# Layer 0's mixture of experts: PSUM banks dealt out anew between the first-layer products and everything else

## The chip, the cores and the metric

The kernel runs on one NeuronCore of a Trainium2 chip. The metric is the device time of one execution in microseconds (us). Engines are named as the profile names them: PE is TensorE (PEld its weight loads), DVE is VectorE, ACT is ScalarE, POOL is GpSimd, SP is SyncE, which issues the DMAs. PSUM has eight banks of 512 float32 columns; TensorE writes them, VectorE and ScalarE read them.

## What is computed

The program is four layers, each an attention part and a feed-forward part with a layer norm before it and a residual after it, on 4096 rows of 128 values. The change touches layer 0's feed-forward part, a mixture of 16 experts on small tokens (each row is 8 tokens of 16 values):

```python
h = x @ Wm + bm
t = h.reshape(bs * L_ * H, HD)                 # 32768 tokens of 16
logits = t @ expert_emb                        # 16 experts
w = jax.nn.softmax(logits, axis=-1)
topw, topi = jax.lax.top_k(w, K)               # K = 2
hmid = jax.nn.gelu(jnp.einsum('td,edi->tei', t, W1) + b1, approximate=False)
eo = jnp.einsum('tei,eio->teo', hmid, W2) + b2
sel = jnp.take_along_axis(eo, topi[:, :, None], axis=1)
comb = (sel * topw[:, :, None]).sum(axis=1)
out = comb.reshape(bs, L_, d)
return out @ Wo + bo
```

## The kernel before

All 16 experts are computed for all tokens, and the gates (zero for the experts that a token did not choose) weight them. The 4096 rows are eight batches of 512 (`NB = 8`, batch `b`). A batch is 8 steps `n` (so `n` runs over 64), and a step is four units `i = 4n + c`. `order()` writes the stage as one list that every engine follows; a step has four slots. The work around the change:

- **mm1** (L248 to L257), one per unit: two bfloat16 matmuls of 512 columns into a pair of PSUM banks. It waits until the GELU of unit i-2 is done, since there are two pairs, banks 0 and 1 and banks 2 and 3. In slot s of step n stands mm1 of unit 4n+5+s.
- **gelu** (L265), one per unit: ScalarE turns a pair of banks into an SBUF buffer (its name in the rows is p1g, xn or xT, by the storage that is used).
- **comb** (L547), two per step, in slots 0 and 1: eight rows of float32 matmuls in four column groups, into bank 4 for the first and bank 5 for the second. It needs all four GELUs of the step, and the bank's last content read.
- **the gating** (L582), one per comb: VectorE reads the comb's bank, adds b2, multiplies by the gates, and so frees the bank.
- **red** (L555), two per group of four steps: matmuls that sum the gated rows, into bank 6. Two groups accumulate in bank 6 and one VectorE copy (L588) takes them out for each batch. Red stands in slot 2 of steps with n % 4 equal to 0 and 1, one in each.
- **finish** (L565, then L188): the product with Wo in bank 7 and VectorE's addition to X.
- **the routing of a batch** ("side" work, a generator with one piece in each slot and two in the first four steps): the transposes *turn* (L179), copy (L299), *wm* (L403), VectorE's *hT* (L306) and the three-part split of h (L309 to L319), *lg* (L409), the maximum and difference (L322, L326), ScalarE's exp (L428), some 13 VectorE operations that find the top two and make the gates (L329 to L376, called rank 0 to 10 after the change), *gateT* (L416) and its copy (L382). All of it goes through bank 7, and turn, the next batch's turn and finish wait for one another there.

Batches 0 and 1 differ. Batch 0's routing is done during layer 0's attention: its loop has 12 rounds, and rounds 4 to 11 each take four pieces (`step(side, 4)`). Rounds 9 to 11 also issue mm1 of units 0 to 6. Batch 1's routing runs at two pieces per slot in steps 0 to 3.

The two lines of mm1 that hold the turnover, and the three of order():

```python
        b, hp, ep, ka = n // 8, n % 4, 4 * (n // 4 % 2) + c, 2 * (i % 2)
        p.wait_ge(k.sem("gelu"), i - 1)
...
                if 7 <= 4 * n + 5 + slot < 256:
                    yield "mm1", 4 * n + 5 + slot
                elif slot == 2 and n > 3 and n % 4 < 2:
```

Of the kernel before, what the change touches and what calls it, by code (L numbers as in the profile page):

```python
# [15 lines left out]
NB = 8  # L16
# [7 lines left out]
def _layout(specs):  # L24
# [166 lines left out]
class Mixture:  # L191
# [3 lines left out]

    def __init__(self, k, ctx):
# [15 lines left out]
        self.gscr = [k.nc.dram_tensor(f"gscr{i}", [128, 512], F32).ap() for i in range(2)]  # L212

# [45 lines left out]
    def gelu(self, a, i):  # L259
        k, ka, ep = self.k, 2 * (i % 2), 4 * (i // 16 % 2) + i % 4  # L260
# [19 lines left out]
    def batch_vector(self, v, b):  # L280
        k, i, at = self.k, b % 2, 4 * (b % 4)
# [15 lines left out]
        v.wait_ge(k.sem("proj"), 3 * b + 3 if b < 4 else 24)
        v.wait_ge(k.sem("wm"), b - 3)
        v.e.tensor_copy(k.xT[:, 128 * at:128 * at + 512], k.ps[:, 7, :]).then_inc(k.sem("xT1").h, 1)  # L299
        yield  # L300
        yield
        yield
        v.wait_ge(k.sem("w", 1), 16)
        v.wait_ge(k.sem("wm"), b + 1)
        v.wait_ge(k.sem("lg"), b - 1)
        v.e.tensor_scalar(hT[:, :], k.ps[:, 7, :], k.Wt(1, "bm"), None, ALU.add).then_inc(k.sem("hT").h, 1)  # L306
        v.wait_ge(k.sem("hT"), b + 1)
        v.wait_ge(k.sem("ts", i), 48 * (b // 2))
        v.e.tensor_copy(tp[0][:, :], hT[:, :]).then_inc(k.sem("tp").h, 1)  # L309
        yield  # L310
        yield
        v.wait_ge(k.sem("tp"), 3 * b + 1)
        v.e.tensor_tensor(tr[:, :], hT[:, :], tp[0][:, :], ALU.subtract).then_inc(v.own.h, v.one())
        tb = v.n
        yield
        v.wait_ge(v.own, tb)
        v.e.tensor_copy(tp[1][:, :], tr[:, :]).then_inc(k.sem("tp").h, 1)
        v.wait_ge(k.sem("tp"), 3 * b + 2)
        v.e.tensor_tensor(tp[2][:, :], tr[:, :], tp[1][:, :], ALU.subtract).then_inc(k.sem("tp").h, 1)  # L319
        yield  # L320
        v.wait_ge(k.sem("lg"), b + 1)
        v.e.tensor_reduce(m1[:, :], lg, AX, ALU.max).then_inc(v.own.h, v.one())  # L322
        t = v.n
        yield
        v.wait_ge(v.own, t)
        v.e.tensor_tensor(D[:, :, :], lg, bc(m1), ALU.subtract).then_inc(k.sem("D").h, 1)  # L326
        yield
        v.wait_ge(k.sem("D"), b + 1)
        v.e.scalar_tensor_tensor(U[:, :, :], D[:, :, :], 0.0, rev, ALU.is_equal, ALU.mult).then_inc(v.own.h, v.one())  # L329
        t = v.n  # L330
        yield
        v.wait_ge(v.own, t)
# [2511 lines left out]
```

## Time and profile before

| | |
|---|---|
| median of 3 runs | 1707.63 us (1703.91 to 1710.57) |
| the profiled execution's own time | 1705.46 us |
| its span, first to last instruction | 1703.7 us |
| mean granted TensorE clock | 0.943 |
| steps 6 to 53 of the stage (start of the first gating of step 6 to that of step 54) | 145.34 to 423.45, 278.11 us |
| starts of the first gatings of steps 55 to 59 | 428.33, 433.21, 438.24, 443.27, 448.15 |
| steps 8k to 8k+3 of the six batches k = 1 to 6 | 22.56, 24.15, 22.56, 24.14, 24.15, 22.56 us |
| stage from the first gating to that of step 63 | 102.51 to 469.78, 367.27 us |

The profile is of one execution. The page gives busy time and its share by engine and in 40 slices; a view by windows gives busy time between two moments; the timeline gives single instructions. A gating (L582) stands once for each comb, so its start times mark the steps. A matmul row's length includes the pipeline's drain, so two starts, not a length, tell how long it keeps PE.

### The profile page before, as it was taken

The numbers are of one execution on the slowest core, as the hardware profiler recorded it, in microseconds if no ns is written. First come the engines' busy times: TensorE is split into PE (matmuls) and PEld (weight loads), VectorE is DVE, ScalarE is ACT, GpSimd is POOL, SyncE is SP. The second block draws the span as 40 slices with busy tenths as digits, with TensorE's granted clock in tenths as the row PEclk, the third lists the DMA queues.
The fourth block names the chain that finished last, engine by engine and source line by source line (L and its number), as shares of the span: only waits on it lengthen the run. The fifth ranks groups of instructions, "written<-read, shape, count | busy, mean of one in ns | idle before, by whom it ended". The sixth has DMA issues, their size and how long they took to land.

```text
span 1703.7 us, 22900 instructions
## 1 busy us (share of the span) xinstructions
PE 1456.3 (85%) x8197; PEld 655.3 (38%) x8235; DVE 1332.1 (78%) x2813; ACT 1040.7 (61%) x1903; POOL 337.0 (20%) x270
## 2 busy tenths in 40 slices
PE   6568898888867867799999999999999898895756
PEld 3522222222246656333333333333333334563645
DVE  7765656666365867788888899888888669998997
ACT  4457878888843121577777787777777675361332
POOL 3000000000011332011111111111111124544554
PEclk9789999999997989999999999999999988898877
DMA  3155545455210010100000000000000000000001
GB/s 88 27 123 123 133 126 132 121 132 132 75 47 1 11 54 1 62 1 1 1 1 1 1 13 13 1 1 1 1 1 1 25 1 1 1 1 0 7 13 31
DMA packets 44657, 64.13 MB, mean 38 GB/s; under 512 B 5376, under 2 KB 26112, under 8 KB 44160
## 3 DMA queue, kind: packets, MB, share of 16 engines
q1 hardware_dynamic: 44544, 62.67, 13.8%
q8 instruction: 65, 1.06, 0.3%
q14 instruction: 48, 0.39, 0.1%
HBM read 54.27 MB, written 7.34 MB: 36 GB/s over the span
## 4 chain that ended last, share of the span: by engine, by line
PE 52%; DVE 26%; issue 11%; ACT 8%; POOL 2%; DMA 1%; SPq 0%; DVEq 0%; POOLq 0%; ACTq 0%
PE ps L1959 11%; PE ps L1950 8%; PE ps L547 6%; PE ps L256 6%; PE ps L1929 4%; DVE p6ac L2501 3%; PE ps L1969 3%; DVE WA L2535 3%; DVE xn L172 2%; PE ps L1939 2%; ACT p1g L265 2%; PE ps L555 1%; PE ps L687 1%; DVE st L154 1%; DVE X L188 1%
## 5 line engine op out<-in xcount | busy, mean ns | idle before, releaser
L2046 ACT ACTIVATE p4E<-ps,p4mx,p4sc 128x512 f32<-128x512 f32 x512 | 392.7, 774 | 138.2 <-DVE p4mx L2005 138.2
L2003 DVE TENSOR_REDUCE p4mx<-ps 128x2 f32<-128x1024 f32 x256 | 312.5, 1221 | 63.7 <-PE ps L1950 61.5
L1959 PE MATMUL ps<-p4E,p4vn 128*64 128x512 f32 x1024 | 249.6, 608 | 9.2 <-POOL p4vn L2064 9.1
L1950 PE MATMUL ps<-p4T 64*128 64x512 f16 x1536 | 200.2, 380 | 3.9 <-ACT p4E L2046 3.2
L582 DVE SCALAR_TENSOR_TENSOR p1Pb<-ps,WB,p1sh 128x512 f32<-128x512 f32 x128 | 96.0, 750 | 131.3 <-PE ps L547 127.0
L256 PE MATMUL ps<-p1R,p1w1s 128*128 128x512 bf16 x474 | 142.4, 392 | 43.9 <-ACT p1g L265 22.2
L166 POOL TENSOR_TENSOR rs<-rs,cst 128x4 f32<-128x4 f32 x58 | 59.9, 1033 | 561.6 <-DVE rs L160 561.6
L2064 POOL TENSOR_TENSOR p4vn<-p4v,p4zs 128x512 f32<-128x512 f32 x64 | 66.7, 1043 | 496.5 <-DVE p4zs L2008 496.5
L265 ACT ACTIVATE p1g<-ps,WB 128x1024 f32<-128x1024 f32 x128 | 136.6, 1113 | 43.6 <-PE ps L256 43.5
L547 PE MATMUL ps<-p1g,WB 128*32 128x512 f32 x512 | 138.3, 629 | 0.0
L547 PE MATMUL ps<-xn,WB 128*32 128x512 f32 x256 | 137.5, 621 | 0.0
L1959 PEld LDWEIGHTS ps<-p4E,p4vn 128*64 128x64 f32 x1024 | 63.6, 136 | 137.0 <-issue 136.9
L1950 PEld LDWEIGHTS ps<-p4T 64*128 64x128 f16 x1536 | 58.9, 94 | 140.5 <-ACT p4E L2046 80.8
L256 PEld LDWEIGHTS ps<-p1R,p1w1s 128*128 128x128 bf16 x512 | 36.4, 99 | 193.3 <-issue 73.7
L1929 PE MATMUL ps<-xT,WA 128*128 128x512 f16 x384 | 104.8, 382 | 2.4 <-DVE X L188 0.9
L2038 ACT ACTIVATE p4T<-ps,p4qkb 128x512 f16<-128x512 f32 x128 | 88.0, 689 | 25.7 <-PE ps L1929 25.0
L2046 ACT ACTIVATION_READ_ACCUMULATOR p4E<-ps,p4mx,p4sc 128x1 f32 x512 | 100.4, 196 | 0.0
L1988 DVE SCALAR_TENSOR_TENSOR p4T<-ps,p4qkb,p4T 128x512 f16<-128x512 f32 x128 | 95.3, 745 | 1.8 <-ACT p4T L2038 1.8
L172 DVE TENSOR_SCALAR xn<-X,mv,rs 128x128 f32<-128x128 f32 x232 | 78.6, 394 | 10.1 <-POOL rs L166 10.0
L188 DVE TENSOR_TENSOR X<-X,ps 128x512 f32<-128x512 f32 x66 | 45.0, 683 | 50.5 <-PE ps L565 16.0
L265 ACT ACTIVATE xT<-ps,WB 128x1024 f32<-128x1024 f32 x64 | 70.9, 1115 | 20.1 <-PE ps L256 20.1
L265 ACT ACTIVATE xn<-ps,WB 128x1024 f32<-128x1024 f32 x64 | 68.9, 1112 | 15.1 <-PE ps L256 15.1
(358 smaller groups left out, 2691.5 us busy)
## 6 DMA issues: line engine op xcount, KB each, us to landing
p1sh<-gscr SPq DMA_DIRECT2D x128, 256.0 KB
p1R<-tscr SPq DMA_DIRECT2D x64, 128.0 KB, 5.2
tscr<-p1tp SPq DMA_DIRECT2D x24, 128.0 KB, 1.7
WA<-in_w SPq DMA_DIRECT2D x1, 2632.0 KB, 8.9
WB<-in_w SPq DMA_DIRECT2D x1, 2560.0 KB, 8.8
X<-in_x SPq DMA_DIRECT2D x8, 256.0 KB, 5.8
gscr<-p1gT SPq DMA_DIRECT2D x8, 256.0 KB, 2.0
out<-X SPq DMA_DIRECT2D x8, 256.0 KB, 2.3
```

Source lines behind the costliest of these rows:

```text
L172: v.e.tensor_scalar(self.xn[:, at + j, :], self.X[:, i, :], self.mv[:, i, 0:1], self.rs[:, i:i + 1], ALU.subtract, ALU.mult).then_inc(self ...
L256: t = p.e.matmul(k.ps[:, ka + hh, :], self.w1s[:, 128 * ep:128 * ep + 128], self.R[b % 2][:, 2 * hp + hh, :], start=True, stop=True)
L265: a.e.activation(self.gb[i % 8], k.ps[:, ka:ka + 2, :].rearrange("p a c -> p (a c)"), ACT.Gelu, bias=k.Wt(1, "b1")[:, ep:ep + 1]).then_inc ...
L547: p.e.matmul(k.ps[32 * c:32 * c + 32, 4 + hh, :], k.Wt(1, "w2")[:, 32 * ep:32 * ep + 32], self.gb[i % 8][:, 512 * hh:512 * hh + 512], star ...
L582: v.e.scalar_tensor_tensor(self.Pb[m % 12][:, :], k.ps[:, 4 + hh, :], k.Wt(1, "b2")[:, half:half + 1], self.GB[n % 4][:, hh, :], ALU.add, ...
L1929: t = p.e.matmul(ps[:, self.bank[what, x], :], pre.part(("kw", "qw")[x[1]], r, slice(128 * hp, 128 * hp + 128)), halves(k, b)[q], start=o ...
L1950: y = p.e.matmul(ps[:, at + hh, :], t[rows, q, 128 * j:128 * j + 128], t[rows, 2 + r, :], start=o == 0, stop=o == 2)
L1959: t = p.e.matmul(ps[64 * hh:64 * hh + 64, 7, :], vn[n % 2][:, j, 64 * hh:64 * hh + 64], E[2 * (n % 2) + hh][:, j, :], start=j == 0, stop=j ...
L1988: v.e.scalar_tensor_tensor(t[:, 2 * c + 1, :], ps[:, self.bank["kq", x], :], pre.qkb[:, 1 - c, hp:hp + 1], t[:, 2 * c, :], ALU.add, ALU.su ...
L2003: v.e.tensor_reduce(m, ps[:, at:at + 2, :], AX, ALU.max).then_inc(v.own.h, v.one())
L2038: a.e.activation(T[n % 2][:, 2 * c, :], ps[:, self.bank[what, x], :], ACT.Identity, bias=pre.qkb[:, 1 - c, n % 8:n % 8 + 1]).then_inc(k.se ...
L2046: a.e.activation(self.E[2 * i + hh][:, j, :], ps[:, at + hh, :], ACT.Exp, bias=self.mx[i][:, j, hh:hh + 1], scale=pre.sc[:, 1, 0:1], accum ...
```

## The change

Units' products get a third pair of banks, 6 and 7: mm1 and gelu use `PAIRS = (0, 2, 6)[i % 3]`, mm1 waits for the GELU of unit i-3, and stands one unit earlier in the list (slot s of step n has unit 4n+6+s). Everything else in the stage (comb, red, turn, wm, lg, gateT, finish, the next layer's turn) takes banks 4 and 5 in turn, in the order in which TensorE meets them: use u goes to bank 4 + u % 2, and waits (`released`) until VectorE has taken out use u-2. For that the side pieces are named and listed (`batch_steps`), and the list is public to all engines.

With it: a red group is closed by itself (bank taken out each group; the second group's is added to the first's in SBUF by a VectorE tensor_tensor), and both reds of a group stand in slots 2 and 3 of the step with n % 4 == 0. Side pieces come ahead of the slot's comb, not behind it. The routing order moves a little: the logits' maximum and difference stand before parts 1 and 2 of the split, and the statistics of the next batch's norm come one step later. Batch 0's routing inside the attention takes its 24 pieces in rounds 4 to 7 (`first`), four non-empty entries in each, where it had rounds 4 to 11; its PSUM uses go to bank 6, and so mm1 of unit 2 waits for batch 0's `gT`.

```diff
+    PAIRS = (0, 2, 6)
...
+        self.bank = {(what, 0): 6 for what in ("turn", "wm", "lg", "gateT")}
+        self.bank.update({u: 4 + i % 2 for i, u in enumerate(uses)})
+        self.last = {u: uses[i - 2] for i, u in enumerate(uses) if i > 1}
...
     def mm1(self, p, i):
-        b, hp, ep, ka = n // 8, n % 4, 4 * (n // 4 % 2) + c, 2 * (i % 2)
+        b, hp, ep, ka = n // 8, n % 4, 4 * (n // 4 % 2) + c, self.PAIRS[i % 3]
-        p.wait_ge(k.sem("gelu"), i - 1)
+        if i % 3 == 2:
+            p.wait_ge(k.sem("gT"), 1)
+        p.wait_ge(k.sem("gelu"), i - 2)
...
+    STEPS = (("rows", 0), ("turn", 3), ("xT", 1), ("wm", 1), ("hT", 0), ("lg", 2), ("logits", 0), ("parts 0", 1), ("parts 1", 0),
+             ("exp", 1), ("rank 0", 0), ("rank 1", 1), ("rank 2", 1), ("rank 3", 0), ("rank 4", 0), ("rank 5", 1), ("rank 6", 0),
+             ("rank 7", 3), ("rank 8", 0), ("rank 9", 1), ("rank 10", 2), ("gateT", 5), ("gT", 0))
...
+    def first(self, n):
+        steps = [labels for labels in self.batch_steps(0) if labels]
+        for labels in steps[4 * n:4 * n + 4 if n < NB - 1 else None]:
+            yield from labels
...
     def order(self):
+        side = self.batch_steps(1)
         for n in range(64):
             for slot in range(4):
-                if 7 <= 4 * n + 5 + slot < 256:
-                    yield "mm1", 4 * n + 5 + slot
+                if 7 <= 4 * n + 6 + slot < 256:
+                    yield "mm1", 4 * n + 6 + slot
+                for _ in range(2 if n < 4 else 1):
+                    yield from next(side, ())
                 if slot < 2:
                     yield "comb", (n, slot)
-                elif slot == 2 and n > 3 and n % 4 < 2:
-                    yield "red", (n // 4 - 1, n % 4)
-                yield "side", 2 if n < 4 else 1
+                elif n > 3 and n % 4 == 0:
+                    yield "red", (n // 4 - 1, slot - 2)
...
+    def released(self, p, use):
+        if use not in self.last:
+            return
+        what, x = self.last[use]
+        if what == "comb":
+            p.wait_ge(k.sem("gated"), 2 * x[0] + x[1] + 1)
+        elif what == "red":
+            p.wait_ge(k.sem("cT"), x + 1)
+        elif what == "turn":
+            p.wait_ge(k.sem("xT1"), x + 1)
+        elif what == "wm":
+            p.wait_ge(k.sem("hT"), x + 1)
+        elif what == "lg":
+            p.wait_ge(k.sem("D"), x + 1)
+        elif what == "gateT":
+            p.wait_ge(k.sem("gT"), x + 1)
...
             elif what == "red":
                 g, hh = x
+                if hh == 0:
+                    self.released(p, (what, g))
                 p.wait_ge(k.sem("gated"), 8 * g + 7 + hh)
-                p.wait_ge(k.sem("cT"), g // 2)
-                               start=g % 2 == 0 and hh == 0, stop=g % 2 == 1 and hh == 1, skip_group_check=True)
+                               start=hh == 0, stop=hh == 1, skip_group_check=True)
...
+                v.wait_ge(k.sem("red"), 8 * g + 8)
+                if g % 2 == 0:
+                    v.wait_ge(k.sem("y1"), g // 2 - 1)
+                    v.e.tensor_copy(cT, k.ps[:, bank[what, g], :]).then_inc(k.sem("cT").h, 1)
+                else:
+                    v.wait_ge(k.sem("cT"), g)
+                    v.e.tensor_tensor(cT, k.ps[:, bank[what, g], :], cT, ALU.add).then_inc(k.sem("cT").h, 1)
...
-                step(side, 4)
+                for what, x in self.mix.first(b):
+                    self.mix.batch_vector(v, what, x)
```

## Rows read from the trace of the kernel before

**Rows 1.** The page: busy us and share of the span; PE's granted clock by slice.

```profile
PE 1456.3 (85%) x8197; PEld 655.3 (38%) x8235; DVE 1332.1 (78%) x2813; ACT 1040.7 (61%) x1903; POOL 337.0 (20%) x270
...
PEclk9789999999997989999999999999999988898877
```

**Rows 2.** Windows: length, busy us by engine (instructions), PE's clock, DMA share, GB/s.

```profile
62.00:102.50 40.50, 27.53 (x171) 22.26 (x172) 28.82 (x63) 9.24 (x9) 2.29 (x2) 0.83 0.31 60
102.51:145.34 42.83, 31.59 (x173) 8.02 (x170) 26.57 (x57) 27.18 (x27) 3.31 (x3) 0.92 0.56 146
145.34:423.45 278.11, 243.79 (x1472) 63.85 (x1500) 173.83 (x316) 225.24 (x211) 12.78 (x11) 0.98 0.51 129
156.90:179.46 22.56, 18.20 (x112) 3.74 (x113) 17.29 (x27) 19.96 (x20) 0.00 (x0) 1.00 0.69 139
179.46:202.46 23.00, 21.56 (x136) 6.87 (x138) 11.89 (x27) 17.49 (x17) 2.29 (x2) 1.00 0.37 124
202.46:226.61 24.15, 19.64 (x111) 3.80 (x113) 17.28 (x27) 19.96 (x20) 0.00 (x0) 0.93 0.63 140
306.00:310.00 4.00, 3.78 (x16) 0.57 (x20) 0.87 (x2) 2.29 (x4) 0.00 (x0) 0.57 0.73 127
428.33:448.15 19.82, 17.96 (x110) 3.71 (x112) 6.70 (x9) 16.95 (x17) 0.00 (x0) 1.00 0.29 106
```

**Rows 3.** Timeline, steps without routing: start, length, engine, line, count, idle before.

```profile
431.46 0.60 PE L256 MATMUL ps<-p1R,p1w1s 128*128 128x512 bf16 x2 [0.78 <-ACT xn L265]
432.00 0.63 PE L547 MATMUL ps<-p1g,WB 128*32 128x512 f32 x3
...
433.00 0.60 PE L256 MATMUL ps<-p1R,p1w1s 128*128 128x512 bf16 x2
...
435.06 1.07 PE L555 MATMUL ps<-p1Pb,cst 128*32 128x512 f32 x8
...
436.06 1.04 PE L256 MATMUL ps<-p1R,p1w1s 128*128 128x512 bf16 x4
436.70 3.13 ACT L265 ACTIVATE p1g<-ps,WB 128x1024 f32<-128x1024 f32 x3 [0.42 <-PE ps L256]
437.03 0.62 PE L547 MATMUL ps<-xn,WB 128*32 128x512 f32 x1
```

**Rows 4.** Timeline, the exp of batch 4 and after it.

```profile
300.80 1.28 ACT L428 ACT_TABLE_LOAD   x1
...
304.04 1.11 ACT L265 ACTIVATE p1g<-ps,WB 128x1024 f32<-128x1024 f32 x1
...
305.21 0.61 PE L256 MATMUL ps<-p1R,p1w1s 128*128 128x512 bf16 x2 [2.09 <-ACT p1g L265]
...
307.05 1.08 PE L547 MATMUL ps<-p1g,WB 128*32 128x512 f32 x3
```

**Rows 5.** Timeline, TensorE alone: pieces of a batch's routing and its finish.

```profile
319.10 0.66 PE L416 MATMUL ps<-cst,p1E 128*128 128x128 f32 x4
...
328.12 1.05 PE L565 MATMUL ps<-WB,p1cT 128*128 128x128 f32 x8
329.01 0.59 PE L256 MATMUL ps<-p1R,p1w1s 128*128 128x512 bf16 x2
...
335.42 1.12 PE L403 MATMUL ps<-xT,WB 128*128 128x512 f32 x2
```

**Rows 6.** VectorE's groups in one batch: line, count, busy us, mean ns.

```profile
L582 DVE SCALAR_TENSOR_TENSOR p1Pb<-ps,WB,p1sh 128x512 f32<-128x512 f32 x17 | 12.8, 750 | 15.3 <-PE ps L547 15.3
...
L354 DVE TENSOR_TENSOR p1U<-p1U,cst 128x512 f32<-128x512 f32 x1 | 0.7, 681 | 0.0
```

**Rows 7.** Timeline, the attention's end and the stage's start.

```profile
94.31 0.69 DVE L382 COPY p1gT<-ps 128x512 f32<-128x512 f32 x1
...
97.61 0.69 DVE L188 TENSOR_TENSOR X<-X,ps 128x512 f32<-128x512 f32 x1 [2.61 <-PE ps L716]
...
102.51 0.75 DVE L582 SCALAR_TENSOR_TENSOR p1Pb<-ps,WB,p1sh 128x512 f32<-128x512 f32 x1 [4.22 <-DMA p1sh<-gscr]
```

More of the change, by code:

```diff
@@ new lines, in batch_scalar, with batch_gpsimd @@
+    def batch_scalar(self, a, what, b):
+        k = self.k
+        if what == "exp":
+            Df, Ef = (x[:, :, :].rearrange("p a c -> p (a c)") for x in (self.D, self.E))
+            a.wait_ge(k.sem("D"), b + 1)
+            a.wait_ge(k.sem("gateT"), b)
+            a.e.activation(Ef, Df, ACT.Exp).then_inc(k.sem("exp1").h, 1)
+    def batch_gpsimd(self, g, what, b):
+        k = self.k
+        if what == "stats":
+            k.ln_rstd(g, "A", 8 + b, b)
+        elif what == "rows":
+            g.wait_ge(k.sem("w", 1), 16)
+            g.wait_ge(k.sem("A", "row"), 4 * (8 + b) + 4)
+            k.bias_rows(g, b, k.Wt(1, "bo"), k.sem("bias1"))
@@ L522, in order @@
             if n + 4 < 64:
                 yield "gates", n + 4
-        yield "side", 99
+        for rest in side:
+            yield from rest
         yield "red", (15, 0)
@@ L527, in order, with uses @@
         yield "finish", 7
+    def uses(self):
+        for what, x in self.order():
+            if what in ("comb", "turn", "wm", "lg", "gateT", "next turn", "finish"):
+                yield what, x
+            elif what == "red" and x[1] == 0:
+                yield what, x[0]
+    def released(self, p, use):
+        k = self.k
+        if use not in self.last:
+            return
+        what, x = self.last[use]
[5 more added lines that the diff above has]
+            p.wait_ge(k.sem("xT1"), x + 1)
+        elif what == "wm":
+            p.wait_ge(k.sem("hT"), x + 1)
+        elif what == "lg":
+            p.wait_ge(k.sem("D"), x + 1)
+        elif what == "gateT":
+            p.wait_ge(k.sem("gT"), x + 1)
+        elif what == "next turn":
+            p.wait_ge(k.sem("A", "xT"), 9)
+        elif what == "finish":
+            p.wait_ge(k.sem("x1"), x + 1)
     def tensor(self, p):
-        k = self.k
-        side = self.batch_tensor(p, 1)
+        k, bank = self.k, self.bank
+        p.wait_ge(k.sem("x0"), NB)
         for what, x in self.order():
@@ L718, in tensor @@
             else:
-                step(side, 4)
+                for what, x in self.mix.first(b):
+                    self.mix.batch_tensor(p, what, x)
                 for n in self.early(b):
@@ L782, in vector @@
             else:
-                step(side, 4)
-        step(side, 99)
+                for what, x in self.mix.first(b):
+                    self.mix.batch_vector(v, what, x)
     def scalar(self, a):
@@ L821, in gpsimd @@
         g.e.tensor_tensor(sc[:, 1, :], sc[:, 0, :], k.C("mhalf")[:, 0:3], ALU.pow).then_inc(k.sem("bnrstd").h, 1)
[L822 removed]
         for s, b in self.order():
             if s == 4:
[L825 to L826 removed]
+                for what, x in self.mix.first(b):
+                    self.mix.batch_gpsimd(g, what, x)
 class Routing:
```

445 lines of the change are left out of this document (182 added, 263 removed), and 2 rows, old and new, of the table AGAIN.

## The prediction

> **What bounds the kernel now.** I read the page first. TensorE is busy 85% of the span, and in the stage of layer 0's experts its clock stands at 9 or above in nearly every slice [rows 1], so the stage runs at the full 2.4 GHz level but for short falls. Next the windows over the stage. Steps 6 to 53, six batches, take 278.11 us, 46.35 a batch [rows 2]. VectorE works 29 us of such a batch (17.29 + 11.89), TensorE's rows cover 40 and ScalarE's 37 [rows 2]; no engine is full. A row's length holds drain, so TensorE's share is better worked from starts.
>
> Starts in steps without routing [rows 3]: an mm1 keeps TensorE for 0.54 us when float32 work follows (431.46 to 432.00), a comb 1.00 (to 433.00), a red 1.00 (435.06 to 436.06), two mm1 in a row 0.97 together (436.06 to 437.03), so 0.43 when another mm1 follows. A step is four mm1 and two combs: 0.43 + 0.97 + 1.00 + 1.54 = 3.94 us. ScalarE's three GELUs in a row take 3.13, of which one alone is 1.11: 1.01 each, 4.02 a step. Yet four steps take 19.82 us [rows 2], where TensorE's own work is 4 x 3.94 + 2 reds at 1.11 (a red, and 0.11 more for the mm1 ahead of it) = 18.0 and ScalarE's 16.1. The reader is to see why at 431.46: TensorE stands idle 0.78 us for a GELU, and ScalarE in its turn 0.42 us for TensorE (436.70). With two pairs of banks each waits for the other: mm1 of unit i may not start before GELU i-2 is done, and only one GELU is then left to cover mm1, comb and red. In steps with a red TensorE is the bound: 3.94 + 1.11 = 5.05, and their gatings lie 5.03 apart; in the others the ping-pong is, at 4.88 (starts of steps 55 to 59, in the table above).
>
> In a batch with routing there is a second loss. ScalarE's exp with two table loads puts 3.24 us between the end of one GELU and the start of the next (300.80 to 304.04) [rows 4]; TensorE runs dry for 2.09 us. After it the granted clock over four us is 0.57 [rows 2], near the 1.2 GHz level, and a comb's rows are 1.08 us long for 0.63 [rows 3, 4]. So steps 16 to 19 take 24.15 us and steps 8 to 11, in which the clock stays up, 22.56 [rows 2]. Of the six batches three are of each kind.
>
> **The change, part by part.** *Third pair, mm1 one unit earlier.* mm1 of unit i waits for GELU i-3, so two GELUs (2.0 us) cover what stands between two mm1, at most 1.54 - 0.54 = 1.0 us of comb or red and the 0.6 of mm1's own length. The ping-pong goes; what is late next is the fuller engine: ScalarE at 4.02 in steps without red, TensorE in the others. The two reds now stand in one step: four times 1.54 = 6.16. Four steps: 6.16 + 3 x 4.02 = 18.2 against 19.82, 1.6 gained.
>
> *Steps 12 to 15 of a batch* (group's reds, finish, turn, wm, lg; 23.00 us now [rows 2]). A routing piece keeps TensorE for its length less the drain of 0.16, as finish shows (1.05 long, the next start 0.89 on) [rows 5]: wm 0.97, gateT 0.50, finish 0.89; turn as gateT or less, 0.44; lg, eight rows of 128 columns like finish, 0.9. The sum: 6.16 + 4.02 + (3.94 + 0.89 + 0.44) + (3.94 + 0.97 + 0.9) = 21.3. Gain 1.7.
>
> *Steps 8 to 11* (split, exp, ranks, gateT; 22.56 and 24.15, mean 23.35). TensorE's work is 6.16 + 3 x 3.94 + 0.50 = 18.5. Here the two turning banks cost something, for VectorE's routing now stands ahead of the gatings that free them. I walk it from the end of lg at time 0. VectorE: maximum and difference to 1.6, the split's three operations to 3.4, gating of comb (8,0) to 4.15 (0.75 each, 0.68 to 0.69 a routing operation [rows 6]). TensorE by then has done mm1, comb (8,0), mm1, comb (8,1), mm1 at 3.6, and red wants the bank of comb (8,0): 0.6 lost. VectorE goes on with rank 0, a gating, ranks 1 to 4 and the group's copy, to 9.1; comb (9,1), ready at 8.8, wants that bank: 0.4 lost. Ranks 7 to 9 lie before gating (10,0), done at 15.9, and comb (11,0) waits some 0.4 for it. ScalarE's 3.24 us fall where TensorE has the two reds and mm1 a lead of three units: GELU 40 ends at 7.6 and mm1 43, which waits for it, stands at 8.3. So TensorE is not dry there and I count no clock fall. Steps 8 to 11: 18.5 + 1.5 = 20.0, gain 3.35.
>
> *Elsewhere a turnover is hidden.* A gating ends 1.0 us after its comb (0.25 + 0.75), and between two uses of a bank TensorE has mm1, comb, mm1: 2.08 us. Likewise xT, hT, D, gT and finish's addition, one VectorE operation each (two for D). The cover is 1.1 us; behind more than one queued VectorE operation it is gone, at 0.7 a further one.
>
> *One more VectorE copy a batch* (0.69): hidden, VectorE is at 29 of 46 us and would be at 30 of 41. SP's list keeps its DMAs and their order among gates, gscr and R loads; at a batch in 41 us DMA's share of 0.53 or so becomes 0.6. No wait there that I can find.
>
> *The head.* Batch 0's 24 pieces go into rounds 4 to 7. VectorE's work is the same, but it meets two waits more (for lg, and for gateT), and rounds 8 to 10 of the attention, empty of routing, run at TensorE and VectorE latency. Its last copy, `gT`, comes at about 94.3 as now [rows 7], but then in round 7 and not in round 11: that round's addition (0.69) and those of rounds 8 to 10 follow, each after a wait for its matmuls that I take at 2.1, a little under the last one's 2.61 [rows 7]. So the last addition ends near 94.3 + 0.7 + 0.7 + 3 x 2.8 = 104, at best 103, where it now ends at 98.3. Part is hidden: the first gating waits 4.22 us for the gates' DMA till 102.51 now [rows 7]. Steps 0 to 5 take 42.83 us, and TensorE works 31.6 of them [rows 2]: the order of batch 1's routing on VectorE sets them. Walked in the new order (a routing operation 0.69, a gating 0.75) step 3 ends within 1 us of now, and steps 4 and 5 then take 10.2 and not 10.1 us but start 1.4 earlier, ScalarE having run ahead. I take step 6 to begin 1.3 us earlier, with bounds from 6 us later (the attention's whole delay) to 4 earlier.
>
> *The tail*, steps 54 to 63: nine steps in 46.3 us, by 7 x 4.02 + 2 x 6.16 + finish, turn and the norm's wait of 2.7 it is 43.2. Gain 3.1.
>
> **The sum.** Per batch 1.7 + 3.35 = 5.05, six times 30.3; I take 0.5 a batch off for waits that the walk misses (one queued VectorE operation more in each): 27.3. With head 1.3 and tail 3.1 it is 31.7. The profiled execution's 1705.46 becomes 1673.8; that execution lies 2.2 below the median of 1707.63, so I say 1676. What follows the stage starts so much earlier and is not otherwise touched. Bounds: TensorE without a wait in the batches (8 x 3.94 + 4 x 1.11 + 3.74 for the pieces = 39.7 each, 40 gained) and 4 at the head, 47 in all: 1661; or 2 us a batch more of turnover waits than I count and 6 lost at the head, 19 less than my gain: 1695.
>
> A row and a rule. The idle 0.78 us before an mm1 [rows 3] is what limits; TensorE's weight loads are busy 23% of the six batches [rows 2]. The Trainium skill (Perfetto Trace Analysis, Identifying the Most-Contended Engine) says that TensorE's matmul busy share tells little of how near it is to its limit, and that weight-load busy time tells more. By that reading TensorE, with weight loads at 63.85 of 278.11 us, would have much room and ScalarE would set the pace.
>
> **Rivals.**
>
> *VectorE binds in steps 8 to 11.* For it: 17.3 us of VectorE work in 22.56 already [rows 2], ahead of the gatings now, and any wait of its own (exp, lg) goes straight to the banks. Then these steps gain nothing: 6 x 1.7 + 3.1 + 1.3 = 14.6, 1693. Against: the walk leaves VectorE 2 us of slack in the four. 0.14.
>
> *ScalarE sets the pace throughout:* 32 x 1.01 + 3.24 = 35.5 a batch, 6 x 10.8 + 5 = 70 gained, 1637. Against it: red steps at 5.03 now fit TensorE's own sum of 5.05, which leaves it no room. 0.05. (So it would come out by the page of the Trainium skill named above.)
>
> *Slower: the two banks turn too slowly everywhere.* In a batch 16 combs, two red groups and five others need a bank, 184 uses in eight batches. For it: the gatings now queue behind routing operations. The gain of 32 and the bound of 8.5 are eaten when each use waits 0.22 us on average, that is when VectorE frees a bank 2.3 us after the use's end and not 1.0: two routing operations queued ahead of every gating. That holds in a quarter of the steps, not in all. At 0.3 each 55 are lost against 32 won: 1731. 0.07.
>
> *No change:* TensorE's starts in step with ScalarE's ends hide a limit of its own, the third pair merely moves idle from before mm1 to before comb, and the stage stays at 46 a batch. Within 0.5% (8.5 us, about what the measurement can tell). 0.06.
>
> **How the numbers follow.** My case has 0.68, its own range 1662 to 1688 (the one bound, and half of the other's losses and a little more). With VectorE binding (0.14) the range is 1660 to 1696; what is left out has 0.18. Faster by over 0.5%: 0.68 + 0.14 + 0.05 = 0.87; within: 0.06; slower: 0.07.
>
> **What would show it.** Gatings four steps apart 18.2 us without routing (19.82 now); ScalarE's GELUs in long unbroken rows; no fall of the clock after exp; batch time 41 to 42. New waits of TensorE on VectorE's gating and on the group copy in steps 8 to 11, 1.5 to 2 us a batch. The attention's last addition some 5 us later. Wrong it would be if TensorE's waits on VectorE passed 5 us a batch, or the head lost over 6.

## The result, and the profile after

The changed kernel took 1662.55 us (median of 4 runs, 1661.80 to 1664.72) where the kernel before took 1705.77 beside it (4 runs, 1703.21 to 1710.57): ratio 0.9745 [0.972, 0.9771]. Predicted were 1676 with a range of 1660 to 1696, so the measured time lies 2.6 us inside the range's lower end. Repeated later beside other runs of the kernel before it gave 0.9739 [0.9715, 0.9764]. The profiled execution took 1664.72 us, its span 1662.9, mean granted clock 0.942.

The page after: busy time, clock by slice, and the groups of the stage's four main operations (count, busy us, mean ns, then the engine's idle time before them).

```profile
PE 1449.5 (87%) x8235; PEld 658.6 (40%) x8235; DVE 1337.0 (80%) x2821; ACT 1032.7 (62%) x1903; POOL 339.3 (20%) x270
...
PEclk9889999999989889999999999999999988897877
...
L265 PE MATMUL ps<-p1R,p1w1s 128*128 128x512 bf16 x512 | 144.8, 384 | 3.7 <-ACT xn L274 2.5
L274 ACT ACTIVATE p1g<-ps,WB 128x1024 f32<-128x1024 f32 x128 | 137.6, 1136 | 13.0 <-PE ps L265 12.3
L574 DVE SCALAR_TENSOR_TENSOR p1Pb<-ps,WB,p1sh 128x512 f32<-128x512 f32 x128 | 94.7, 748 | 57.8 <-PE ps L542 56.7
...
L542 PE MATMUL ps<-xn,WB 128*32 128x512 f32 x256 | 135.4, 612 | 0.3 <-DVE p1Pb L574 0.3
```

The idle time before mm1 (L265; L256 before) is 3.7 us in all, before the largest GELU group 13.0, before the gatings 57.8 (they were 43.9, 43.6 and 131.3 in the page of before).

Windows of the changed kernel's trace, with the columns of [rows 2]: steps 0 to 5, the six batches (steps 6 to 53), steps 8 to 11, steps 12 to 15, one whole batch (steps 16 to 23), four steps without routing.

```profile
106.75:145.33 38.58, 31.67 (x177) 8.00 (x170) 26.06 (x51) 27.85 (x27) 2.86 (x3) 0.91 0.62 143
145.33:386.12 240.79, 238.06 (x1501) 65.20 (x1500) 176.12 (x317) 219.44 (x212) 12.29 (x11) 1.00 0.58 149
156.96:174.50 17.54, 17.08 (x107) 3.92 (x106) 15.36 (x26) 17.50 (x18) 0.00 (x0) 1.00 0.74 150
174.50:197.09 22.59, 22.59 (x146) 6.94 (x144) 14.35 (x32) 18.96 (x19) 2.31 (x2) 1.00 0.42 147
197.09:237.22 40.13, 39.67 (x252) 10.88 (x250) 29.71 (x56) 36.46 (x36) 2.31 (x2) 1.00 0.57 149
390.05:408.05 18.00, 18.00 (x113) 3.72 (x112) 6.70 (x9) 16.47 (x17) 0.00 (x0) 1.00 0.37 117
```

Read against [rows 2], 278.11 us have become 240.79, and TensorE's rows now cover 238.06 of them and not 243.79 of 278: it is full. ScalarE has 219.44, VectorE 176.12. The clock is 1.00 in place of 0.98. Four steps without routing take 18.00 where they took 19.82. The two parts of a batch, 17.54 and 22.59, are divided by the start of a gating, and at step 16 (as at step 8) that gating (197.09, below) starts 1.8 us after its comb's last rows end (194.74 and 0.60), because VectorE is at the split; work of the one part counts in the other, and only their sum of 40.13 is to be compared, with 46.35. Marked by TensorE's own start of each step's first comb, the two parts take 19.13 and 21.00 us, where before they took 23.35 (mean of the six batches) and 23.00.

### The profile page after: what moved, and what is told of

It is laid out like the page before. It is cut to its first block, busy times and chain, and to the rows that moved or that the text cites. A ratio compares the mean times of both kernels' runs of the same rounds, so it can differ in the third digit from the quotient of the medians.

```text
span 1662.9 us, 22946 instructions
## 1 busy us (share of the span) xinstructions
PE 1449.5 (87%) x8235; PEld 658.6 (40%) x8235; DVE 1337.0 (80%) x2821; ACT 1032.7 (62%) x1903; POOL 339.3 (20%) x270
## 3 DMA queue, kind: packets, MB, share of 16 engines
q1 hardware_dynamic: 44544, 62.67, 14.1%
## 4 chain that ended last, share of the span: by engine, by line
PE 55%; DVE 28%; issue 10%; ACT 4%; POOL 2%; DMA 0%; DVEq 0%; SPq 0%; POOLq 0%; ACTq 0%
PE ps L1957 11%; PE ps L1948 8%; PE ps L265 7%; PE ps L542 7%; PE ps L1927 4%; DVE p6ac L2499 4%; PE ps L1967 3%; DVE WA L2533 3%; PE ps L1937 2%; DVE xn L172 2%; PE ps L551 2%; PE ps L688 1%; DVE X L188 1%; DVE st L154 1%; POOL p4vn L2062 1%
## 5 line engine op out<-in xcount | busy, mean ns | idle before, releaser
L265 PE MATMUL ps<-p1R,p1w1s 128*128 128x512 bf16 x512 | 144.8, 384 | 3.7 <-ACT xn L274 2.5
L574 DVE SCALAR_TENSOR_TENSOR p1Pb<-ps,WB,p1sh 128x512 f32<-128x512 f32 x128 | 94.7, 748 | 57.8 <-PE ps L542 56.7
L265 PEld LDWEIGHTS ps<-p1R,p1w1s 128*128 128x128 bf16 x512 | 35.8, 97 | 156.8 <-issue 58.4
L1967 PE MATMUL ps<-WA,p4cx 128*128 128x128 f32 x512 | 74.1, 288 | 0.8 <-DVE p4cx L2010 0.8
```

What stands on the lines that cost most here:

```text
L265: t = p.e.matmul(k.ps[:, ka + hh, :], self.w1s[:, 128 * ep:128 * ep + 128], self.R[b % 2][:, 2 * hp + hh, :], start=True, stop=True)
L574: v.e.scalar_tensor_tensor(self.Pb[m % 12][:, :], k.ps[:, bank[what, x], :], k.Wt(1, "b2")[:, half:half + 1], self.GB[n % 4][:, hh, :], AL ...
L1967: t = p.e.matmul(ps[:, 6, 128 * j:128 * j + 128], self.cx[x % 2][:, 128 * j:128 * j + 128], k.Wt(4, "lw")[:, 128 * hp:128 * hp + 128], sta ...
```

## Where the time went

Timeline of the changed kernel at the exp of batch 2 (answers to [rows 4]; weight loads left out).

```profile
192.88 1.05 PE L421 MATMUL ps<-WB,p1hT 128*128 128x128 f32 x8
...
194.74 0.60 PE L542 MATMUL ps<-p1g,WB 128*32 128x512 f32 x3
...
197.07 1.28 ACT L438 ACT_TABLE_LOAD   x1
197.09 0.74 DVE L574 SCALAR_TENSOR_TENSOR p1Pb<-ps,WB,p1sh 128x512 f32<-128x512 f32 x1
...
197.88 1.06 PE L551 MATMUL ps<-p1Pb,cst 128*32 128x512 f32 x8 [0.46 <-DVE p1Pb L574]
...
198.36 0.63 ACT L438 ACTIVATE p1E<-p1D 128x512 f32<-128x512 f32 x1
198.88 0.61 PE L265 MATMUL ps<-p1R,p1w1s 128*128 128x512 bf16 x2
...
199.01 1.28 ACT L274 ACT_TABLE_LOAD   x1
199.42 1.06 PE L551 MATMUL ps<-p1Pb,cst 128*32 128x512 f32 x8
...
200.31 3.13 ACT L274 ACTIVATE p1g<-ps,WB 128x1024 f32<-128x1024 f32 x3
200.42 0.61 PE L265 MATMUL ps<-p1R,p1w1s 128*128 128x512 bf16 x2
...
200.95 0.62 PE L542 MATMUL ps<-xn,WB 128*32 128x512 f32 x1
...
201.77 0.68 DVE L584 TENSOR_TENSOR p1cT<-ps,p1cT 128x512 f32<-128x512 f32 x1
...
202.37 0.68 DVE L388 TENSOR_TENSOR p1U<-p1D,p1m 128x512 f32<-128x512 f32 x1
```

The exp and two table loads still keep ScalarE from its GELUs for 3.24 us (197.07 to 200.31), but TensorE has the end of an mm1, red, mm1 and red in that time, goes on with mm1 at 200.42 and starts comb at 200.95. The one idle of TensorE in the batch is the 0.46 us before the first red, for the bank that the late gating (197.09) frees: the first turnover wait of the walk, there put at 0.6. The waits view of that batch (line waited for, sum, times, longest; PEld is the weight load that goes ahead of the matmul, and its wait is no loss while TensorE still works) has one wait of TensorE itself for VectorE, and the others are of weight loads:

```profile
PEld ps L542 <- DVE p1Pb L574: 1.2, 2, 0.8
...
PEld ps L551 <- DVE p1Pb L574: 0.9, 1, 0.9
...
PE ps L551 <- DVE p1Pb L574: 0.5, 1, 0.5
PEld ps L542 <- DVE p1cT L584: 0.4, 1, 0.4
PEld ps L542 <- DVE p1D L358: 0.4, 1, 0.4
```

Steps without routing, timeline of the changed kernel (answers to [rows 3]):

```profile
389.10 2.12 ACT L274 ACTIVATE p1g<-ps,WB 128x1024 f32<-128x1024 f32 x2
...
391.09 2.13 ACT L274 ACTIVATE xn<-ps,WB 128x1024 f32<-128x1024 f32 x2
391.37 1.51 PE L265 MATMUL ps<-p1R,p1w1s 128*128 128x512 bf16 x6
...
393.08 2.15 ACT L274 ACTIVATE xT<-ps,WB 128x1024 f32<-128x1024 f32 x2
```

The GELUs of xT at 393.08 follow those of xn at 391.09 and of p1g at 389.10 with no idle mark, and TensorE's rows have none either. Before, both had one in every turn [rows 3].

The head, VectorE alone (answers to [rows 7]):

```profile
92.68 0.69 DVE L370 COPY p1gT<-ps 128x512 f32<-128x512 f32 x1 [1.27 <-PE ps L429]
...
102.63 0.69 DVE L188 TENSOR_TENSOR X<-X,ps 128x512 f32<-128x512 f32 x1 [2.02 <-PE ps L716]
...
106.75 0.75 DVE L574 SCALAR_TENSOR_TENSOR p1Pb<-ps,WB,p1sh 128x512 f32<-128x512 f32 x1
```

The last addition ends 5.0 us later (it started at 97.61), the first gating starts 4.24 later (5.28 in a second profile of the changed kernel), and step 6 starts at 145.33 where it started at 145.34. The stage's account, from starts of gatings: head 0.0 gained, six batches 37.3, steps 54 to 63 (46.33 down to 41.51) 4.8; the last step's gating comes at 427.63 and not at 469.78, 42.1 earlier.

## The experiments

Twelve kernels ran. "Stage's end" below is the start of step 63's first gating: 469.78 before, 427.63 in the changed kernel. Between that and the end of the span these kernels take 1233.5 to 1239.6 us, so a difference of a few us in total time isn't resolved, while starts inside the stage repeat to 0.02 us from step 4 on (the changed kernel's second profile has step 6 at 145.32 and step 63 at 427.61, though its first gating comes 1.04 us later, at 107.79). Where the text speaks of a step's length by TensorE, it is from the start of its first comb to that of the next step.

**One: the new order with two pairs.** The changed kernel with banks 6 and 7 left out of mm1's use:

```diff
-        b, hp, ep, ka = n // 8, n % 4, 4 * (n // 4 % 2) + c, self.PAIRS[i % 3]
+        b, hp, ep, ka = n // 8, n % 4, 4 * (n // 4 % 2) + c, self.PAIRS[i % 2]
-        if i % 3 == 2:
-            p.wait_ge(k.sem("gT"), 1)
-        p.wait_ge(k.sem("gelu"), i - 2)
+        p.wait_ge(k.sem("gelu"), i - 1)
...
-                    yield "mm1", 4 * n + 6 + slot
+                    yield "mm1", 4 * n + 5 + slot
```

> The changed kernel with two pairs of banks for the units' products (0 and 1, 2 and 3), the wait for GELU i-2 and the list's old place of mm1; all else as changed (two banks turning over, both reds in one step, batch 0's routing in rounds 4 to 7). Theory: the third pair is the whole gain, so the ping-pong returns at 4.88 us in steps without a red; the step with both reds stays at 6.16, which makes four steps without routing 6.2 + 3 x 4.88 = 20.8 us, 1.0 more than the 19.82 of the kernel before, and the time 1705 to 1722 us. Rival: the new order and the turning banks are themselves a gain, and the time stays below 1690.

Measured: 1694.66 us (1693.09 to 1698.08), ratio 0.992 [0.9891, 0.9949], stage's end 455.34. Steps without routing are as the theory has them, 4.88 and 6.13 us, but the total is not, and it isn't under the rival's 1690 either: a batch takes 43.99 us. Windows of it, one batch, columns as above:

```profile
201.41:245.40 43.99, 40.32 (x251) 10.75 (x250) 29.96 (x56) 37.29 (x36) 2.30 (x2) 1.00 0.55 135
```

So the two turning banks and the new order are no burden that the third pair has to pay for; they bring 14.4 us at the stage's end alone, of which 14.1 in the six batches. The third pair with its lead brings the other 27.7. Three things make up the 2.35 us a batch. The exp, which costs 3.5 us a batch before (experiment five), costs 1.6 here: the step with exp and both reds takes 7.71 us by TensorE, one with both reds alone 6.13. The two reds in one step cost 1.9 (four steps without routing take 20.77 us for 19.82, twice a batch). What is left, 2.3 us less for the other pieces of routing, is worked out and not taken apart by a run.

**Two: three pairs, but mm1 no earlier in the list.**

```diff
-                if 7 <= 4 * n + 6 + slot < 256:
-                    yield "mm1", 4 * n + 6 + slot
+                if 7 <= 4 * n + 5 + slot < 256:
+                    yield "mm1", 4 * n + 5 + slot
```

> The changed kernel with three pairs, but mm1 one unit later in the list, as before (slot s of step n has unit 4n+5+s). Theory: the lead in the list is a part of the gain: a comb needs the step's last GELU, which needs an mm1 that now stands only two mm1 ahead of it, and TensorE waits some 0.3 to 0.4 us there in the 48 steps without a red: 1674 to 1682 us, those steps at about 4.35 us instead of 3.96. Rival: the third pair alone does it and the place in the list is worth nothing: 1660 to 1666.

Measured: 1674.80 (1669.15 to 1675.13), ratio 0.9792 [0.9766, 0.9819]. Steps without routing 4.32 us. Timeline of such a step:

```profile
392.55 4.13 ACT L274 ACTIVATE p1g<-ps,WB 128x1024 f32<-128x1024 f32 x4 [0.42 <-PE ps L265]
...
393.30 0.62 PE L542 MATMUL ps<-xn,WB 128*32 128x512 f32 x1
...
393.71 0.62 PE L542 MATMUL ps<-p1g,WB 128*32 128x512 f32 x1
```

The comb's column group that needs the last GELU (p1g, 393.71) starts 0.41 us after the others (393.30): comb now waits for GELUs. That is the theory's mechanism, but not in all 48 steps without a red: by TensorE steps 17 to 19 take 0.3 to 0.4 us longer than in the changed kernel, and steps 21 to 23, with finish, turn, wm and lg, no longer at all. A batch takes 41.18 us for 40.13, and the stage's end comes at 433.88, 6.3 us later (6.4 in the six batches, 1.8 in the tail, and the head 1.9 earlier). So of the 27.7 us the one unit of lead is 6.3. That the median of 1674.80 lies 12 us over the changed kernel's is not explained by it: the profiled execution took 1669.15, the other three 1674.5 to 1675.1.

**Three: batch 0's routing spread out again, over rounds 4 to 10.**

```diff
-        steps = [labels for labels in self.batch_steps(0) if labels]
+        steps = list(self.batch_steps(0))
```

> The changed kernel, with batch 0's routing spread over the attention's rounds 4 to 10 again (four entries of the list a round, empty ones counted). Theory: packing it into rounds 4 to 7 put the attention's last addition 4 to 5 us later (102.6 against 97.6); with the spread it comes back to about 98, the gates' DMA or VectorE's routing of batch 1 then sets the start, and 1 to 5 us are gained: 1657 to 1661. Rival: the delay is all hidden behind the DMA of the gates and batch 1's routing, and the time is the same within 1 us.

Measured: 1664.10 (1663.65 to 1666.66), ratio 0.9741 [0.9718, 0.9763]. VectorE's rows at the head:

```profile
96.74 0.69 DVE L370 COPY p1gT<-ps 128x512 f32<-128x512 f32 x1 [0.39 <-PE ps L429]
99.37 0.69 DVE L188 TENSOR_TENSOR X<-X,ps 128x512 f32<-128x512 f32 x1 [1.94 <-PE ps L716]
...
105.50 1.41 DVE L574 SCALAR_TENSOR_TENSOR p1Pb<-ps,WB,p1sh 128x512 f32<-128x512 f32 x2 [1.93 <-DMA p1sh<-gscr]
```

The last addition is 3.3 us earlier (4 to 5 were expected), but the gates are finished 4.1 us later (96.74 for 92.68), and the first gating now waits 1.93 us for their DMA. The stage's end is 424.81, 2.8 us earlier, and the rest of the kernel, 1237.9 us, gives no sign of it in total. The theory is right in the stage (1 to 5 us earlier) and wrong in the total.

**Four: routing pieces behind comb and red again.** The side loop's two lines go behind them.

```diff
-                for _ in range(2 if n < 4 else 1):
-                    yield from next(side, ())
                 if slot < 2:
                     yield "comb", (n, slot)
                 elif n > 3 and n % 4 == 0:
                     yield "red", (n // 4 - 1, slot - 2)
+                for _ in range(2 if n < 4 else 1):
+                    yield from next(side, ())
```

> The changed kernel, with the routing's pieces behind the slot's comb or red and not ahead of it. Theory: TensorE has work for 39.7 of a batch's 40.1 us, the banks turn in time either way, and the order is worth little: within 3 us of the changed kernel, 1659 to 1666. Rival: the gatings' place behind routing operations on VectorE holds the banks back; then this order gains or loses over 8 us.

Measured: 1678.36 (1677.92 to 1680.65), ratio 0.9824 [0.9801, 0.9846], stage's end 439.70. The rival holds: the order is worth 12 us, 2.4 by step 4, 1.4 in each batch and 1.2 in the tail. By TensorE the 1.4 stand in one step of the batch, step 23, with 7.10 us for 5.68. The waits view of one batch (steps 16 to 23):

```profile
PEld ps L542 <- DVE xT L344: 1.5, 1, 1.5
PE ps L542 <- DVE xT L344: 1.0, 1, 1.0
```

Turn comes at 233.03 there, then a comb (234.00), then the comb that wants turn's bank. VectorE's copy of turn (235.88) now stands in the list behind the gating (235.21) of the comb between them, so that the second comb starts only at 236.61, 1.0 us late. With the pieces ahead of comb the copy stands ahead of that gating.

**Five and six: a GELU in the exp's place,** in the kernel before and in the changed one. No table has to be loaded for it; the gates' values are others.

```diff
-        a.e.activation(Ef, Df, ACT.Exp).then_inc(k.sem("exp1").h, 1)
+        a.wait_ge(k.sem("w", 1), 16)
+        a.e.activation(Ef, Df, ACT.Gelu, bias=k.Wt(1, "b1")[:, 0:1]).then_inc(k.sem("exp1").h, 1)
```

> The kernel before, with ScalarE's exp of the routing replaced by a GELU with a bias: the gates get other values, and the two table loads round each exp go (2.56 us a batch of ScalarE). Theory: before the change the 3.24 us of exp and loads lie open, and cost a fall of TensorE's clock in three of six batches: steps 8k to 8k+3 lose 2.5 to 3 us of their 22.56 or 24.15, the clock stays up, and the time is 1684 to 1692. Rival: the exp is not what stretches these steps but VectorE's routing is; then under 5 us are gained.

> The same replacement in the changed kernel (the gates get other values, the table loads go). Theory: after the change the exp falls where TensorE has two reds and a lead of three units, and is hidden: at most 2 us are gained, 1660 to 1663. Rival: ScalarE's 3.24 us still cost part of their length in each batch: over 6 us gained.

Measured: in the kernel before 1689.24 (1685.14 to 1690.36), ratio 0.9889 [0.986, 0.9919], stage's end 448.03, 21.8 us earlier; the step with the exp takes 5.04 us where it took 7.77 and more, and a batch 42.83 for 46.35. In the changed kernel 1667.81 (1667.16 to 1668.89), ratio 0.9762 [0.9738, 0.9786], stage's end 427.48, 0.15 earlier. So half of what the change gains is what the exp had cost. In the changed kernel a batch takes 39.95 us for 40.13: the exp still costs 0.2 us a batch, 1.1 in the six, and the stage's end hides it because step 6 starts 0.95 later. The profiled execution of six took 4.2 us more in total than the changed kernel's, behind the stage (1239.6 us for 1235.3); the cause wasn't found.

**Seven and nine: the two reds together in the old order,** ahead of the exp, and one step later, behind it. In the kernel before:

```diff
-                elif slot == 2 and n > 3 and n % 4 < 2:
-                    yield "red", (n // 4 - 1, n % 4)
+                elif n > 3 and n % 4 == 0:
+                    yield "red", (n // 4 - 1, slot - 2)
```

and nine with `elif n > 4 and n % 4 == 1:` in that line's place.

> The kernel before (two pairs, its banks and list), with both reds of a group in slots 2 and 3 of the step with n % 4 equal to 0, as the change has them. Theory: with two pairs this costs, since that step is TensorE's at 6.16 us and the other three stay at the ping-pong's 4.88: 20.8 us for four steps and not 19.82. The exp stands three slots later (step 8k+1, slot 0), behind both reds, so its 3.24 us lie open as before: 1715 to 1725. Rival: the gain of the run with two pairs in the new order (1694.7) comes from the reds standing together; then this is under 1700.

> The kernel before, with both reds of a group in slots 2 and 3 of the step with n % 4 equal to 1, right behind the exp (step 8k+1, slot 0). Theory: what the new order brings with two pairs is that the two reds, 2 us of TensorE that need no GELU, fall into ScalarE's 3.24 us: TensorE's dry time goes from 2.1 to about 1 us and the clock does not fall; 1698 to 1706, and 12 to 22 us faster than the run with the reds ahead of the exp. Rival: the place of the reds against the exp is worth nothing: the same as that run.

Measured: seven 1718.46 (10 runs, 1713.78 to 1722.63), ratio 1.0054 [1.0037, 1.0072], 47.7 us a batch, as expected; nine 1715.00 (10 runs, 1708.76 to 1717.95), ratio 1.0031 [1.0014, 1.0049], 46.59 a batch. Nine should have been 12 to 22 us faster than seven and is 3.5. Its exp step takes 7.9 us, but that step now has both reds in it, and such a step takes 6.14 without exp: the exp costs 1.8 us there. Before, the exp step takes 7.77 with one red and 5.03 without exp, 2.7, and in three of six batches 1.6 more for the fallen clock. So the reds' place behind the exp does halve what the exp costs, from 3.5 to 1.8 us a batch, and keeps the clock up, as the theory had it. Against before, this is eaten by both reds standing in one step, 1.9 a batch. Against seven, where the exp costs 3.8, a batch gains only 1.1: by TensorE steps 20 to 23, in which finish now falls into the step of the reds, take 24.04 us for 23.06. Another 2.9 us are lost at the head and in the tail. The timeline of nine shows what stays open; its second table load is at 213.69:

```profile
212.84 0.61 PE L256 MATMUL ps<-p1R,p1w1s 128*128 128x512 bf16 x2
...
213.38 1.07 PE L555 MATMUL ps<-p1Pb,cst 128*32 128x512 f32 x8
...
216.15 0.60 PE L256 MATMUL ps<-p1R,p1w1s 128*128 128x512 bf16 x2 [1.71 <-ACT p1g L265]
```

TensorE does a comb and one red (213.38) under the exp. The second stands behind an mm1, and with two pairs that mm1 waits for the GELU that the exp holds back: 1.71 us dry. In experiment one, with two pairs as well, the exp starts one piece nearer to the reds (its first table load at 201.44), and both stand under it:

```profile
202.20 1.07 PE L549 MATMUL ps<-p1Pb,cst 128*32 128x512 f32 x8 [0.40 <-DVE p1Pb L572]
203.20 0.60 PE L263 MATMUL ps<-p1R,p1w1s 128*128 128x512 bf16 x2
203.74 1.07 PE L549 MATMUL ps<-p1Pb,cst 128*32 128x512 f32 x8
205.85 0.60 PE L263 MATMUL ps<-p1R,p1w1s 128*128 128x512 bf16 x2 [1.04 <-ACT p1g L272]
```

TensorE is dry for 0.40 and 1.04 us, and the exp costs 1.6. In both kernels TensorE does two pieces of 1.0 us and one mm1 between them under the exp, and then waits.

**Ten: the reds one step later in the changed kernel.**

```diff
-                elif n > 3 and n % 4 == 0:
+                elif n > 4 and n % 4 == 1:
```

> The changed kernel, with both reds of a group one step later (n % 4 equal to 1), so that a step lies between exp (step 8k, slot 1) and reds. Theory: the lead of three units alone does not cover ScalarE's 3.24 us; TensorE runs dry for 1 to 1.5 us in each of seven batches: 1668 to 1675. Rival: TensorE's list is full anyway and the reds' place is worth nothing: 1661 to 1665.

Measured: 1682.24 (1679.80 to 1684.76), ratio 0.9843 [0.9815, 0.9872], more than expected. Windows (two batches, then the 4 us from the end of the dry spell and 4 us in the batch before it) and timeline of it:

```profile
157.11:200.41 43.30, 40.15 (x247) 11.10 (x251) 30.07 (x56) 36.76 (x36) 2.30 (x2) 0.96 0.55 137
200.41:242.62 42.21, 39.08 (x248) 11.05 (x251) 30.08 (x57) 36.66 (x36) 2.31 (x2) 1.00 0.56 140
163.00:167.00 4.00, 3.67 (x19) 0.60 (x20) 3.53 (x6) 2.77 (x4) 0.00 (x0) 0.65 1.16 117
204.80:208.80 4.00, 3.59 (x22) 0.65 (x22) 3.90 (x7) 3.96 (x4) 0.00 (x0) 1.00 1.16 131
```

```profile
204.80 0.61 PE L265 MATMUL ps<-p1R,p1w1s 128*128 128x512 bf16 x2 [2.19 <-ACT p1g L274]
...
225.72 1.06 PE L551 MATMUL ps<-p1Pb,cst 128*32 128x512 f32 x8
```

Without reds to do, TensorE is dry for 2.19 us at the exp though it has three pairs. Where the reds now stand, red, red and finish (225.72, 227.25, 228.25) follow one another with at most one mm1 between two of them, and ScalarE is idle 1.40 us, but TensorE is not held up by it: by its own steps the crowding costs 0.09 us and the exp 2.07 over the changed kernel. So with three pairs the reds' place does matter. The exp's price a batch, from the length of its step by TensorE less that of such a step without exp, and the fallen clock with it (before and changed: the batch less that of five and of six), is:

| | exp costs a batch | clock falls |
|---|---|---|
| two pairs, both reds ahead of the exp (seven) | 3.8 us | in all six batches |
| two pairs, the reds in two steps (before) | 3.5 us | in three of six |
| two pairs, a comb and one red under the exp (nine) | 1.8 us | in none |
| two pairs, both reds under the exp (one) | 1.6 us | in none |
| three pairs, no red near the exp (ten) | 2.2 us, and 1.1 more with a fall | in three of six |
| three pairs, both reds under the exp (changed) | 0.2 us | in none |

Neither the third pair nor the reds' place hides the exp alone; together they do.

**Eight: the kernel before with its routing pieces ahead of comb,** nothing else changed.

```diff
+                yield "side", 2 if n < 4 else 1
                 if slot < 2:
...
-                yield "side", 2 if n < 4 else 1
```

> The kernel before, with the routing's pieces ahead of the slot's comb and not behind it, as the change has them. Theory: some waits of routing on TensorE and VectorE get shorter, as the changed kernel loses 12 us of the stage with the pieces behind; the exp's place hardly moves, so a few us: 1698 to 1708. Rival: this is the whole of what the new order brings with two pairs: 1692 to 1697.

Measured: 1696.41 (1690.24 to 1700.12), ratio 0.992 [0.9893, 0.9946], stage's end 454.94. The rival's range holds it and the theory's doesn't. The total is that of experiment one (0.992 and 455.34), but it is another gain: of 14.8 us at the stage's end 6.9 are at the head (step 4 comes at 128.38 for 135.28), 6.4 in the six batches and 1.6 in the tail, where one has 0.1, 14.1 and 0.2. That the totals are equal is a coincidence. A batch takes 45.29 us on average for 46.35; three of the six have a fall of the clock as before, and one without takes 44.57 for 45.56. By TensorE 0.9 of this 1.0 us is gained in the last two steps, with turn, wm and lg (10.62 for 11.56); lg's wait of 0.64 us for hT is gone. The exp's step is as long as before (7.76). In steps 0 to 5 the granted clock is 1.00 for 0.92, so how much of the head's 6.9 is the order and how much the clock isn't parted. The profiled execution (1690.24) is also the fastest of the five.

**Eleven and twelve: a head with its own bank.** Batch 0's routing spread as in three, batch 1's routing in bank 6 too, and units 0 to 17 on two pairs, beside the changed kernel once more.

```diff
-        self.bank = {(what, 0): 6 for what in ("turn", "wm", "lg", "gateT")}
+        self.bank = {(what, b): 6 for what in ("turn", "wm", "lg", "gateT") for b in (0, 1)}
...
+        return self.PAIRS[i % 2] if i < 18 else self.PAIRS[i % 3]
```

> The changed kernel with another head: batch 0's routing spread over rounds 4 to 10 of the attention, batch 1's turn, wm, lg and gateT in bank 6 for themselves (no turnover with combs in steps 0 to 3), and so only two pairs for units 0 to 17; the third pair joins when batch 1's gT is done. Theory: in the changed kernel the head costs, for the first turn waits for a gating and that for the gates' DMA; with a bank of its own step 4 starts at 128.5 to 130.5 and not at 135.3, all later steps as now: 5 to 6.5 us under the changed kernel that runs beside it. Rival: VectorE's routing of batch 1 sets the head in any case, and it is the 2.8 us of the run with the spread alone, or nothing in the end.

> The changed kernel itself, beside the one with another head, so that the two are compared on one chip: ratio 0.974 to 0.976 to the kernel before, with the stage's starts and deltas as in its first profile.

Measured: 1662.89 (1659.91 to 1665.39), ratio 0.9724 [0.9697, 0.9751], against 1663.47 (1661.86 to 1667.28), 0.9739 [0.9715, 0.9764]. Step 4 comes at 132.82 and not at 128.5 to 130.5, the stage's end at 425.19, 2.4 us earlier than the changed kernel, which is what the spread alone gives (three: 132.52 and 424.81). So batch 1's own bank brought nothing that shows; since units 0 to 17 had only two pairs here, it isn't shown that the turning banks cost nothing at the head. No version was found that is measurably faster than the changed kernel.

## Why the prediction held, and where it was off

*The mechanism* was as predicted: the mutual wait of TensorE and ScalarE in steps without red goes (18.00 us for four steps; predicted 18.2), the exp is hidden behind the two reds but for 0.2 us (the first timeline, experiment six), the clock stays up, VectorE binds nowhere, a batch is near TensorE's own sum (39.7 worked out, 40.13 measured). Of the rivals, a VectorE that binds, ScalarE as pace, slow turning and no change are all out. The Trainium skill (Perfetto Trace Analysis, Identifying the Most-Contended Engine) would have TensorE's distance from its limit read from the share of peak matmul work, which was not worked out here, and from the weight loads' busy time, and not from the matmuls' busy time. In the full batch the weight loads have 10.88 of 40.13 us, and TensorE's matmuls 39.67. Here the sum of start intervals told it, and the weight loads' share did not.

*The size.* Predicted gain at the stage's end 31.7 us, measured 42.1. Steps 8 to 11 were put at 20.0 us and steps 12 to 15 at 21.3; by TensorE they take 19.13 and 21.00. Term by term:

| term | predicted | measured |
|---|---|---|
| turnover waits, a batch | 1.5 in the walk and 0.5 on top | 0.5 |
| six batches | 27.3 | 37.3 |
| steps 54 to 63 | 3.1 | 4.8 |
| head | 1.3 (bounds -6 and 4) | 0.0 |

The mis-sized step is the turnover waits of steps 8 to 11. The walk had three (0.6, 0.4, 0.4) and an allowance; only the first is there, at 0.46. It laid VectorE's operations end to end at their lengths, 0.69 and 0.75, but nine successive starts (197.09 to 202.37) lie 0.66 apart on average, and the casts of the split take 0.43: the group's copy, put at 9.1 us after lg's end and needed at 8.8, ended at 8.5 (202.45 from 193.93). Another 0.08 in some of the steps without red is ScalarE's pace of 4.02, which I had bind there: the GELUs' starts at 389.10, 391.09 and 393.08 lie 1.99 apart for two units, so the pace is 3.98, and the steps take 3.93 to 3.97, close to TensorE's sum of 3.94. Three of the recorded sums are off by a little, with no effect on the result: the walk's waits (0.6, 0.4, 0.4) make 1.4 and stand in the sum as 1.5, the pieces make 3.70 and not 3.74, and ScalarE's 32 units with the exp 35.6 and not 35.5. In the tail the pieces beside the steps cost 1.6 and not 2.7.

*The head*: the attention's delay came out as said (last addition 103.3, predicted 103 to 104), and steps 0 to 5, in 38.58 us for 42.83, made up for all of it and no more. The 1.4 us by which steps 4 and 5 were to start earlier aren't there: step 4 starts at 135.26 for 135.28.

*Behind the stage* the changed kernel's profiled execution took 1.4 us longer, so that 1673.8 predicted met 1664.7.

*What I had not seen* is the order within a slot. The prediction took the place of the routing pieces only as something that delays gatings, and gave it no gain. Eight shows that it brings 0.8% (14 us) in the old kernel without any other edit, four that it brings 12 in the new one. One's expectation failed for more than that: the new order with two pairs also halves what the exp costs, which I had tied to the third pair. The prediction's gain thus rests on a sum of TensorE's work that is right however the waits were removed, not on a full account of what removed them.

*Left open:* where the 2.3 us a batch come from that experiment one saves in the other pieces of routing (eight's order alone saves 1.0 in a batch), how much of eight's head is its order, and why six is longer behind the stage.

## What to carry to other kernels

Where two engines hand buffers back and forth, sum each engine's start intervals over a period; if neither reaches the period's length, a third buffer together with one more unit of lead is worth what lies between; the third buffer without the lead gave only part of it here (experiment two). In a list that all engines follow, put a piece whose result another engine must read ahead of the long operation and not behind it, and try that edit first: it costs a line. Put work that needs nothing of the engine about to be away (here the reds) where it will be away. With two buffers this halved the price of the absence (3.5 us to 1.6 or 1.8 a batch) and cost as much again by crowding the work into one step; with a third buffer and its lead the absence was all but hidden (0.2). And where two edits give the same total, compare their stages before calling them one cause: experiments one and eight did not gain in the same place.

## What the runs showed of the hardware

TensorE's clock did not fall after every dry spell of one length. In experiment ten TensorE is dry for 2.19 us before mm1 at 204.80 and as long (2.18) in the batch before it; there the four us at 163 have a granted clock of 0.65, near the 1.2 GHz level, and the batch takes 43.30, while after 204.80 the clock stays at 1.00 and the batch takes 42.21. Windows over the next three batches have 0.96, 1.00 and 0.96. The kernel before has the same picture: a dry spell of 2.09 us or a little more (2.32 at most) in all six batches and the fall in three [rows 2, 4]. A fall cost 1.6 us there and 1.1 in ten. In seven TensorE is dry for 2.50 us and all six batches have a fall (a clock of 0.95 or 0.96 over each); in nine it is dry for 1.71 to 1.93 us, in one for 1.04, and none has. What picks the batches in the kernel before and in ten isn't known. In the changed kernel, where TensorE isn't dry, none of the six batches has a fall (1.00 over all of them).
